# A new order of all steps in a fused two-block kernel, loop bounds read in three parts, and four more unread first products

## Chip, core and metric

One Trainium2 chip, one core. The time is the device time of the whole program in microseconds (us). The rows below come from one profiled execution; the median is over three unprofiled ones.

## What is computed

Two blocks, each a sequence mixer `s` gated by a mixture of experts `g`, on x of 16 x 256 x 128 (4096 tokens, float32):

```python
xn = layernorm(x)
s = linear_attention(xn)        # relu(q)+eps, relu(k)+eps, per sequence of 256
g = silu(moe0(xn))              # 8 experts of width 64, exact gelu, top 2, weights' sum
x = x + s * g
xn = layernorm(x)
s = ttt(xn)                     # per token: W -= LR*outer(2/d*(W k + b - v), k); out = W q + b
g = silu(moe1(xn))              # 8 experts of width 512, exact gelu, top 2, normalised
return x + s * g
```

In block 0 all eight experts are computed for every token. In block 1 each token goes only through the two experts chosen for it.

## The kernel before

**Groups.** The 4096 tokens are 32 tiles of 128, in 8 groups of 4. Each group passes through some fifty named steps. A step "3 kT" is group 3's share of the step kT; each engine has its own branch for it in its own `work(step, g)`, with the waits on semaphores that it needs, or nothing. Block 0: stats, roots, ln0, xt0, v, lg0, floor, sel, q, k, selT, kv, att, hid0 0 to 3 (dense experts), tok, y0, bias0, mix0. Block 1's mixer: ln1, norm1, xt1, resid, lg1, kT, qT, gram_n, diag and base and back (16 x 16 diagonal blocks of a triangular matrix go to HBM, are inverted on DVE and come back), half4, join4, half5, join5, turn, half6, join6 (the inverse by doubling: PE product, ACT copy into pn, PE product, copy back), gram_q, gram_x, then the chain u1, cross, u2, out, each a PE product and a copy that the next needs. "turn" is four transposes (L976) and one ACT copy (L1214); "half6" is L929 and the ACT copy L1198; "join6" L937 and L1204.

**Routing.** "rank", "slots" and "tok" give each token its two places in the HBM tensor `routed` (a region for each expert) and its weights. "send 0" to "send 3" are POOL's: each issues two indirect DMAs (L690) and waits first until the previous send of the group has landed. "7 send 0" waits for "9 tok" (weights_ready), since the gates of block 1 lag by two. "7 slots" also makes the table of loop bounds (L1601) on DVE. "U fill" is SP's: eight writes (L540) of filler rows behind each expert's tokens.

**Units.** Block 1's experts work on units of 256 routed rows. "U load k" is SP's load of a unit into a ring of four (it waits for unit k-4 to be done with: ring_free). "U hid k" is PE's hidden layer (L1025) and the transposition of unit k+1 (L1015), with DVE taking unit k+2 out of the ring (L1606). "U out k" is PE's output layer (L1048, in the loops L1037), ACT's four gelus of unit k+1 (L1235), DVE's scaling of the results, POOL's two indirect writes to `results` (L699). Units 0 to 7 are of fixed number and interleaved with the groups; the rest run in one loop per expert whose bounds each engine reads out of the table. PE reads its bounds two at a time in its "U hid" steps; ACT and DVE read all nine after "U out 6"; SP after the first pass. SP starts the load of unit 8 only when all sends of all groups have landed ("U sent", rows_landed) and the fill too. At the end the two results of each token are added by PE and the outputs stored.

**The order.** All engines walk one tuple, `ORDER` (L78 to L125). An engine works strictly in that order, so a step that waits holds up all behind it on the same engine. "idle" steps are four products of the identity into a bank that nobody reads (L742); eleven such steps stand in the order, and `FIRST_IDLE` (8) more products come before PE's first wait for weights (w_nat, L749).

Of the kernel before, what the change touches and what calls it, by code (L numbers as in the profile page):

```python
# [66 lines left out]
HALF = P // 2  # L67

GATES_LAG = 2
FIRST_IDLE = 8  # L70
IDLE = 4

WIDE = (0, 1, 6, 7)
# [2 lines left out]
ROOTS_TO = {0: 1, 1: 3, 3: 8}  # L76

ORDER = (  # L78
# [47 lines left out]

# [3 lines left out]
def two_block_kernel(nc, x, W_qkv, W_out, b_out, gate_w, w1_0, b1_0, w2_0, b2_0,  # L130
                     theta_K, theta_V, theta_Q, W0, b0, Wg, W1, b1, W2, b2, out):
    seqs, seq_len, D = x.shape
    E = gate_w.shape[1]
# [13 lines left out]
    FIRST_ALL = FIRST_UNITS * E  # L147
# [23 lines left out]
    with ctx:  # L171
        def sb(name, shape, dt=F32):
            return ctx.enter_context(nc.sbuf_tensor(name, shape, dt))
# [24 lines left out]
        cb0 = sb("cb0", [P, D])  # L198
# [19 lines left out]
        fill = sb("fill", [P, 2, HALVES, ROW])  # L218
# [34 lines left out]
        selT = [sb(f"selT_{i}", [P, P], BF16) for i in range(2)]  # L253
# [13 lines left out]
        send = [sb(f"send{i}", [P, CHOICES, TILES, ROW]) for i in range(2)]  # L267
# [7 lines left out]
        kT = sb("kT", [P, GW])  # L275
        qT = sb("qT", [P, GW])
# [154 lines left out]
        def unit_bounds(eng, first=0, last=E + 1):  # L431

            eng.wait_ge(table_ready, 1)
            return [eng.value_load(table[0:1, e:e + 1], min_val=FIRST_ALL, max_val=MAX_UNITS)
                    for e in range(first, last)]
# [299 lines left out]
        def _(pe):  # L735
# [3 lines left out]
            def idle_products(n, to=psC[:, 1, 0:P]):  # L739

                for _ in range(n):
                    mm(to, ident[:, :], ident[:, :], start=True, stop=True)  # L742

            pe.wait_ge(ident_in, 1)
            idle_products(FIRST_IDLE)
            pe.wait_ge(consts, 1)
# [346 lines left out]
        def _(act):  # L1093
# [148 lines left out]
            def unit_work(what, k=0):  # L1242
                if what == "first":
                    turned(0)
                elif what == "hid":
                    turned(k + 1)
                elif what == "gelu":
                    gelus(0, 0)
                elif what == "out":
                    gelus(k + 1, (k + 1) % E)  # L1250
                    if k == FIRST_ALL - 2:
                        bounds.extend(unit_bounds(act))

            bounds = []
            first_pass(act, work, unit_work)
# [11 lines left out]
        def _(dve):  # L1267
            v = nc.vector
# [369 lines left out]
            def unit_work(what, k=0):  # L1638
                if what == "first":
                    take(0)  # L1640
                    dve.wait_ge(S["xuT_ps"], 1)
                    take(1)
                elif what == "hid":
                    take_ahead(k)
                elif what == "out":
                    results_of(k, k % E, tiles(psB[:, 1, :], HALVES))
                    if k == FIRST_ALL - 2:
                        bounds.extend(unit_bounds(dve))

            bounds = []  # L1650
            first_pass(dve, work, unit_work)
# [45 lines left out]
```

## Time and profile before

| | us |
|---|---|
| median of 3 runs | 464.46 (461.81 to 465.18) |
| profiled execution | 466.61 |
| its span | 464.9 |
| PE, DVE, ACT, POOL busy | 418.2, 284.0, 215.4, 155.8 |
| mean granted clock of TensorE | 0.974 |

PE is the matmul engine, DVE VectorE, ACT ScalarE, POOL GpSimd, SP the queue that issues most DMAs. Times are microseconds from the start of the span. A timeline row gives start, duration, engine, line, operation and tiles, the count of merged instructions, and in brackets the idle time of the engine just before and what ended it. A float32 product of a 128-wide tile leaves two records. L12 is line 12 of the kernel.

### The profile page before, as it was taken

What the parts mean: (1) busy time and instruction counts of PE and PEld (TensorE: products, weight loads), DVE (VectorE), ACT (ScalarE), POOL (GpSimd) and SP (SyncE); (2) the same over time, 40 slices, a digit from 0 to 9 for tenths busy, and PEclk for the clock granted to TensorE, in tenths of its full rate; (3) what the DMA queues carried; (4) which work ended last, traced back from release to release, by engine and by line L of the source; (5) the groups of instructions that cost most, each with busy time, mean ns of one, the idle gap of its engine ahead of it and who ended that gap; (6) DMA issues with size and microseconds to landing.
All of it is one profiled execution on the core that took longest, in us unless ns stands there. A gap on an engine that the chain in (4) does not pass through costs nothing. (4 is left out here: it accounts for less than half of the span.)

```text
span 464.9 us, 9785 instructions
## 1 busy us (share of the span) xinstructions
PE 418.2 (90%) x2912; PEld 352.1 (76%) x2912; DVE 284.0 (61%) x1137; ACT 215.4 (46%) x525; POOL 155.8 (34%) x215
## 2 busy tenths in 40 slices
PE   6989988999999999998987989489799999999873
PEld 5967666878878889687776879388689899998631
DVE  2688889887887889888757476103133344343327
ACT  3274546555544746524425343214256555555512
POOL 6420014024034231533242014513344455555410
PEclk9999999999999999999999989779899999999998
DMA  7379011363172231121223213411122222222577
GB/s 187 105 147 168 8 37 35 75 196 87 33 199 75 83 75 38 42 77 43 63 55 91 50 32 91 117 45 45 47 61 66 70 69 75 68 70 70 147 253 216
DMA packets 63426, 40.80 MB, mean 88 GB/s; under 512 B 18324, under 2 KB 56088, under 8 KB 63384
## 3 DMA queue, kind: packets, MB, share of 16 engines
q1 hardware_dynamic: 58688, 31.27, 27.2%
q0 software_dynamic: 4352, 8.99, 5.8%
q8 instruction: 21, 0.34, 0.3%
q14 instruction: 21, 0.17, 0.1%
q10 hardware_dynamic: 344, 0.03, 0.1%
HBM read 21.78 MB, written 18.48 MB: 87 GB/s over the span
## 5 line engine op out<-in xcount | busy, mean ns | idle before, releaser
L690 POOL DMA_INDIRECT routed<-send,slot x64 | 65.0, 1015 | 128.3 <-DMA routed<-send,slot 50.6
L699 POOL DMA_INDIRECT results<-nat,y_to x72 | 70.1, 974 | 107.0 <-DVE nat L1634 85.1
L1025 PE MATMUL psA<-xuT,w_all 128*128 128x256 f32 x288 | 71.3, 391 | 3.7 <-ACT h1T L1235 3.2
L1235 ACT ACTIVATE h1T<-psA,b1T 128x256 f32<-128x256 f32 x144 | 62.8, 475 | 15.8 <-PE psB L1048 12.7
L1025 PEld LDWEIGHTS psA<-xuT,w_all 128*128 128x128 f32 x288 | 52.0, 195 | 12.5 <-ACT h1T L1235 3.6
L1606 DVE TENSOR_SCALAR xu<-ring 128x256 f32 (+1 forms) x38 | 11.3, 298 | 80.4 <-DMA ring<-routed 56.0
L1037 PE MATMUL psC<-w_all,h1T 128*128 128x128 f32 x464 | 57.1, 276 | 0.9 <-DVE nat L1618 0.9
L1037 PEld LDWEIGHTS psC<-w_all,h1T 128*128 128x128 f32 x464 | 54.5, 193 | 1.5 <-ACT h1T L1235 1.1
L1226 ACT ACTIVATE xuT<-psB 128x256 f32<-128x256 f32 x37 | 14.2, 384 | 63.4 <-PE psB L1015 38.2
L839 PE MATMUL psB<-xnT,w_l 128*128 128x512 f32 x64 | 34.2, 615 | 0.5 <-ACT selT L1155 0.5
L851 PE MATMUL psB<-w_l,hg0T 128*128 128x128 f32 x256 | 32.9, 281 | 0.0
L1166 ACT ACTIVATE hg0T<-psB,b1T 128x512 f32<-128x512 f32 x32 | 22.0, 689 | 22.7 <-PE psB L841 20.8
L851 PEld LDWEIGHTS psB<-w_l,hg0T 128*128 128x128 f32 x256 | 31.1, 192 | 1.8 <-ACT hg0T L1166 1.4
L841 PEld LDWEIGHTS psB<-selT,expert_of 128*128 128x128 bf16 x128 | 9.8, 98 | 18.2 <-issue 18.2
L1634 DVE TENSOR_SCALAR nat<-nat,y_wt 128x128 f32 (+1 forms) x72 | 17.5, 284 | 7.8 <-issue 4.8
L1173 ACT ACTIVATE gg<-psB,tok_w 128x128 f32<-128x128 f32 x32 | 9.1, 369 | 25.7 <-PE psB L852 21.9
L679 POOL COPY send<-send 128x512 f32<-128x512 f32 x8 | 4.9, 613 | 43.8 <-ACT send L1101 29.5
L742 PE MATMUL psC<-ident 128*128 128x128 f32 x104 | 16.7, 321 | 1.7 <-POOL ident L594 1.7
L742 PEld LDWEIGHTS psC<-ident 128*128 128x128 f32 x104 | 15.6, 234 | 1.7 <-POOL ident L594 1.7
L1321 DVE BATCH_NORM_STATS2 stats<-x_all 128x6 f32<-128x128 f32 x64 | 13.8, 278 | 3.9 <-DMA x_all<-in_L_attn_x_dram 3.7
L1101 ACT ACTIVATE send<-x_all,shift,rstd 128x128 f32<-128x128 f32 x32 | 13.2, 483 | 5.1 <-DVE shift L1338 5.1
L1048 PE MATMUL psB<-w_all,h1T 128*128 128x128 f32 x112 | 15.2, 295 | 0.0
(289 smaller groups left out, 865.0 us busy)
## 6 DMA issues: line engine op xcount, KB each, us to landing
ring<-routed SPq DMA_DIRECT2D x38, 130.0 KB
inv<-inv_room SPq DMA_DIRECT2D x8, 512.0 KB
w_all<-results SPq DMA_DIRECT2D x15, 256.0 KB, 4.5
routed<-ring SPq DMA_DIRECT2D x24, 130.0 KB, 6.1
n_room<-nT SPq DMA_DIRECT2D x8, 256.0 KB
w_all<-in_L_ffn_W_dram SPq DMA_DIRECT2D x1, 2048.0 KB
out_dram<-x_all SPq DMA_DIRECT2D x8, 256.0 KB, 2.3
results<-nat,y_to POOLq DMA_INDIRECT x72
```

Source lines behind the costliest of these rows:

```text
L690: pool.indirect_dma_start(routed[:, :], bass.IndirectOffsetOnAxis(ap=slot[par][:, c, t:t + 1], axis=0), send[par][:, c, t, :], None).then_ ...
L699: pool.indirect_dma_start(results[:, :], bass.IndirectOffsetOnAxis(ap=y_to[:, par, a:a + 1], axis=0), yw[:, par, a, :], None).then_inc(S[f ...
L742: mm(to, ident[:, :], ident[:, :], start=True, stop=True)
L839: mm(psB[:, j % 2, :], w, xT0[:, :], start=True, stop=False)
L851: mm(o, hg0T[:, j, col(t)], w2_l0[:, j, :], start=(j == 0), stop=False)
L1025: last = mm(psA[:, j // 2, (j % 2) * UNIT:(j % 2 + 1) * UNIT], w1_all[:, e, j * P:(j + 1) * P], xuT[:, :], start=True, stop=True)
L1037: last = mm(psC[:, a, 0:D], h1T[:, k, a * P:(a + 1) * P], w2_all[:, f * JF + k, :], start=(k == 0), stop=(k == JF - 1))
L1048: last = mm(psB[:, 1, col(a)], h1T[:, k, a * P:(a + 1) * P], w2_all[:, u % E * JF + k, :], start=(k == 0), stop=(k == JF - 1))
L1166: f(hg0T[:, j, :], psB[:, j % 2, :], ACT.Gelu, bias=b1T[:, HT + j:HT + j + 1]).then_inc(S["hg0_ready"], 1)
L1226: f(xuT[:, :], psB[:, 0, 0:UNIT], ACT.Copy).then_inc(S["xuT_ready"], 1)
L1235: f(h1T[:, j, :], psA[:, j // 2, (j % 2) * UNIT:(j % 2 + 1) * UNIT], ACT.Gelu, bias=b1T[:, n:n + 1]).then_inc(S["gelu_ready"], 1)
L1634: last = v.tensor_scalar(yw[:, mine, a, :], yb[:, a:a + 1, :], y_wt[:, a:a + 1], None, ALU.mult)
```

## The change

`FIRST_IDLE` is 12. ACT and DVE read three of the nine bounds after each of "U out 4", "U out 5" and "U out 6". `ORDER` is another permutation of the same entries; its start and its last part are shown, with the part in between left out. The hunk on the bounds is ACT's (L1251); DVE's (L1647) is the same with `dve`.

```diff
-FIRST_IDLE = 8
+FIRST_IDLE = 12
...
 ORDER = (
-    "0 stats", "0 roots", "0 landed", "0 ln0", "0 wout", "0 xt0", "0 wv", "0 weights", "0 products", "0 v",
-    "0 idle", "0 lg0", "1 idle", "0 floor", "0 sel", "0 q", "0 k", "1 stats", "2 idle", "0 selT", "2 stats",
-    "0 kv", "1 roots", "3 idle", "0 hid0 0", "0 hid0 1", "1 ln0", "3 stats", "0 att", "4 stats", "0 b2",
-    "0 hid0 2", "0 tok", "1 xt0", "4 idle", "1 v", "0 hid0 3", "1 lg0", "0 bias0", "2 ln0", "1 floor",
...
-    "7 floor", "4 send 3", "5 landed", "6 bias0", "3 cross", "5 copies", "7 sel", "6 hid0 3", "7 q", "7 tok",
-    "3 u2", "6 y0", "6 mix0", "3 out", "5 rank", "4 back", "5 slots", "5 kT", "7 selT", "5 send 0", "4 half4",
-    "5 gram_n", "4 join4", "4 half5", "5 diag", "6 ln1", "5 qT", "7 k", "4 join5", "5 gram_q", "6 norm1",
-    "6 xt1", "5 send 1", "4 turn", "7 kv", "4 half6", "4 join6", "4 u1", "5 base", "5 send 2", "7 att",
-    "5 back", "6 resid", "6 lg1", "5 gram_x", "4 cross", "5 send 3", "8 floor", "6 landed", "4 u2", "6 copies",
-    "7 hid0 0", "8 sel", "8 tok", "4 out", "6 rank", "6 slots", "6 kT", "7 hid0 1", "6 gram_n", "5 half4",
-    "6 diag", "5 join4", "6 send 0", "7 hid0 2", "5 half5", "7 bias0", "7 hid0 3", "6 send 1", "5 join5",
-    "6 base", "5 turn", "7 y0", "6 send 2", "5 half6", "6 qT", "5 join6", "6 send 3", "7 mix0", "5 u1",
-    "5 cross", "7 ln1", "6 gram_q", "6 back", "5 u2", "6 gram_x", "7 landed", "U load 0", "U load 1",
-    "7 norm1", "U load 2", "5 out", "U load 3", "7 xt1", "U first", "6 half4", "7 resid", "7 lg1", "U hid 0",
-    "7 kT", "6 join4", "7 gram_n", "U gelu 0", "9 floor", "7 copies", "6 half5", "9 sel", "7 diag", "U hid 1",
-    "6 join5", "U out 0", "U load 4", "7 base", "6 turn", "U hid 2", "6 half6", "6 join6", "6 u1", "U out 1",
-    "6 cross", "7 rank", "U load 5", "7 back", "7 slots", "U hid 3", "9 tok", "6 u2", "U out 2", "6 out",
-    "U load 6", "U hid 4", "7 send 0", "7 half4", "7 join4", "7 send 1", "U out 3", "7 send 2", "U load 7",
-    "7 half5", "7 send 3", "U sent", "7 qT", "7 join5", "7 gram_q", "7 turn", "7 half6", "7 join6", "7 gram_x",
-    "7 u1", "U fill", "U hid 5", "7 cross", "7 u2", "7 out", "U out 4", "U hid 6", "U out 5", "U hid 7",
-    "U out 6",)
+    "0 landed", "0 stats", "0 roots", "0 ln0", "1 stats", "0 wout", "0 wv", "0 xt0", "0 weights", "0 products",
+    "2 stats", "0 v", "0 lg0", "0 floor", "0 idle", "0 sel", "0 k", "0 q", "1 idle", "0 selT", "0 cb0",
+    "1 roots", "0 b2", "0 kv", "0 hid0 0", "1 ln0", "2 idle", "0 att", "3 stats", "0 hid0 1", "0 hid0 2",
+    "0 tok", "4 stats", "0 bias0", "3 idle", "1 xt0", "0 hid0 3", "5 stats", "6 stats", "0 copies", "1 v",
+    "0 y0", "1 lg0", "1 floor", "1 sel", "1 k", "1 q", "2 ln0", "7 stats", "4 idle", "1 kv", "5 idle",
...
+    "5 landed", "7 lg0", "3 u1", "6 hid0 3", "3 cross", "7 floor", "6 bias0", "5 copies", "7 q", "4 back",
+    "7 sel", "3 u2", "6 y0", "4 gram_x", "5 rank", "7 tok", "6 mix0", "3 out", "7 selT", "5 kT", "4 half4",
+    "5 slots", "5 gram_n", "5 send 0", "5 diag", "4 join4", "6 ln1", "5 qT", "4 half5", "7 k", "4 join5",
+    "6 norm1", "5 gram_q", "7 kv", "5 base", "4 turn", "5 send 1", "4 half6", "5 gram_x", "4 join6",
+    "5 send 2", "6 xt1", "5 send 3", "4 u1", "6 landed", "4 cross", "7 att", "6 resid", "5 back", "4 u2",
+    "6 qT", "6 lg1", "6 copies", "8 floor", "8 sel", "8 tok", "4 out", "6 rank", "6 slots", "6 kT", "7 hid0 0",
+    "6 send 0", "6 gram_n", "6 gram_q", "5 half4", "5 join4", "7 hid0 1", "5 half5", "5 join5", "6 send 1",
+    "7 hid0 2", "6 diag", "5 turn", "6 base", "7 hid0 3", "5 half6", "7 bias0", "6 send 2", "7 y0", "5 join6",
+    "7 mix0", "6 back", "5 u1", "6 send 3", "7 landed", "6 gram_x", "5 cross", "5 u2", "7 ln1", "U load 0",
+    "U load 1", "U load 2", "U load 3", "5 out", "7 norm1", "6 half4", "U first", "7 xt1", "6 join4",
+    "7 resid", "7 lg1", "U hid 0", "7 kT", "9 floor", "6 half5", "7 gram_n", "6 join5", "9 sel", "U gelu 0",
+    "U hid 1", "6 turn", "7 copies", "U out 0", "6 half6", "7 diag", "U load 4", "7 base", "U hid 2", "7 back",
+    "6 join6", "6 u1", "6 cross", "U out 1", "7 rank", "7 slots", "U load 5", "U hid 3", "6 u2", "U out 2",
+    "U load 6", "U fill", "6 out", "U hid 4", "7 half4", "U out 3", "7 join4", "U load 7", "7 half5", "7 qT",
+    "9 tok", "7 join5", "7 send 0", "U hid 5", "7 turn", "7 half6", "7 send 1", "7 gram_q", "7 join6",
+    "7 gram_x", "7 send 2", "7 send 3", "U sent", "7 u1", "7 cross", "7 u2", "7 out", "U out 4", "U hid 6",
+    "U out 5", "U hid 7", "U out 6",)
...
                     gelus(k + 1, (k + 1) % E)
-                    if k == FIRST_ALL - 2:
-                        bounds.extend(unit_bounds(act))
+                    if k > FIRST_ALL // 2 - 1:
+                        bounds.extend(unit_bounds(act, len(bounds), len(bounds) + (E + 1) // 3))
```

## Rows read from the trace of the kernel before

**Rows 1.** The page's granted clock of TensorE, in tenths, 40 slices of 11.6 us
```profile
PEclk9999999999999999999999989779899999999998
```

**Rows 2.** Windows: us; busy of PE, PEld, DVE, ACT, POOL; granted clock; DMA share; GB/s
```profile
60.00:80.00 20.00, 17.07 (x117) 12.45 (x116) 16.83 (x66) 11.70 (x29) 7.47 (x8) 1.00 0.13 38
...
295.00:300.00 5.00, 1.57 (x14) 1.18 (x12) 0.69 (x1) 0.38 (x1) 3.78 (x5) 0.75 0.44 130
```

**Rows 3.** Timeline of PE, ACT and DVE, units 7 to 11
```profile
324.64 1.99 PE L1025 MATMUL psA<-xuT,w_all 128*128 128x256 f32 x8 [0.32 <-issue]
...
331.05 3.23 PE L1025 MATMUL psA<-xuT,w_all 128*128 128x256 f32 x8 [2.41 <-ACT h1T L1235]
...
336.56 2.27 PE L1025 MATMUL psA<-xuT,w_all 128*128 128x256 f32 x8
...
340.67 2.15 PE L1025 MATMUL psA<-xuT,w_all 128*128 128x256 f32 x8
...
322.57 0.38 ACT L1226 ACTIVATE xuT<-psB 128x256 f32<-128x256 f32 x1 [1.64 <-PE psB L1015]
...
329.88 0.38 ACT L1226 ACTIVATE xuT<-psB 128x256 f32<-128x256 f32 x1 [4.57 <-issue]
...
323.39 0.29 DVE L1606 TENSOR_SCALAR xu<-ring 128x256 f32<-128x256 f32 x1 [1.99 <-DMA ring<-routed]
...
331.25 0.29 DVE L1606 TENSOR_SCALAR xu<-ring 128x256 f32 x1 [5.80 <-issue]
```

**Rows 4.** Timeline of PE, "U out 2" and "U out 4"
```profile
280.00 1.95 PE L1048 MATMUL psB<-w_all,h1T 128*128 128x128 f32 x16
...
313.61 1.95 PE L1048 MATMUL psB<-w_all,h1T 128*128 128x128 f32 x16
```

**Rows 5.** Timeline of PE, group 7's turn, half6, join6, and "U hid 5"
```profile
295.05 0.41 PE L976 MATMUL psD<-ident,inv 64*64 64x64 f32 x4
...
298.01 1.11 PE L929 MATMUL psD<-inv,nT 64*64 64x64 f32 x8 [2.55 <-issue]
...
302.44 1.08 PE L937 MATMUL psD<-inv,pn 64*64 64x64 f32 x8 [3.31 <-ACT pn L1198]
...
306.17 2.68 PE L1025 MATMUL psA<-xuT,w_all 128*128 128x256 f32 x8
```

**Rows 6.** Timeline of ACT, the copies of group 7's turn and half6
```profile
297.58 0.38 ACT L1214 ACTIVATE inv<-psD 64x256 f32<-64x256 f32 x1 [4.14 <-remote]
...
301.91 0.38 ACT L1198 ACTIVATE pn<-psD 64x256 f32<-64x256 f32 x1 [3.96 <-remote]
```

**Rows 7.** Timeline of SP and POOL, "U fill" and the last send's first half
```profile
293.13 11.08 SPq L540 DMA_DIRECT2D routed<-fill  x8
...
302.43 0.97 POOL L690 DMA_INDIRECT routed<-send,slot  x1 [1.83 <-DMA routed<-send,slot]
```

**Rows 8.** Timeline of DVE, the last write of the table
```profile
282.24 0.15 DVE L1601 CAST table<-bound_f 1x9 int32<-1x9 f32 x1
```

**Rows 9.** Timeline of PE, places at 24, 208 to 219 and 273 us
```profile
24.62 1.11 PE L821 MATMUL psA<-kv,q0T 128*128 128x129 f32 x8
...
208.65 1.10 PE L953 MATMUL psD<-inv,nT 128*128 128x64 f32 x8 [1.12 <-DVE inv L1572]
...
217.36 0.65 PE L937 MATMUL psD<-inv,pn 64*64 64x64 f32 x8 [0.56 <-ACT pn L1198]
...
219.02 1.93 PE L821 MATMUL psA<-kv,q0T 128*128 128x129 f32 x8
...
273.54 3.54 PE L1048 MATMUL psB<-w_all,h1T 128*128 128x128 f32 x16
```

**Rows 10.** Timeline of PE, the first products and the first transposes
```profile
1.73 3.78 PE L742 MATMUL psC<-ident 128*128 128x128 f32 x16 [1.73 <-POOL ident L594]
...
6.81 1.09 PE L749 MATMUL psD<-ident,nat 128*128 128x128 f32 x4 [1.30 <-DMA nat<-in_L_attn_W_dram]
```

**Rows 11.** Waits of POOL: total us, times, longest us
```profile
POOL routed L690 <- DMA routed<-send,slot: 50.6, 23, 6.2
```

More of the change, by code:

```diff
@@ L1646, in unit_work @@
                     results_of(k, k % E, tiles(psB[:, 1, :], HALVES))
-                    if k == FIRST_ALL - 2:
-                        bounds.extend(unit_bounds(dve))
+                    if k > FIRST_ALL // 2 - 1:
+                        bounds.extend(unit_bounds(dve, len(bounds), len(bounds) + (E + 1) // 3))
             bounds = []
```

51 rows, old and new, of the table ORDER are left out of this document.

## Prediction

> **What bounds the kernel now.** I read the page first, then TensorE (PE) in stretches, then the timelines at the places where it stood still. PE is busy 418.2 us of the span of 464.9, so all that a new order can win is in the other 46.7 us and in products at half clock. The clock line of the page [rows 1] shows where its granted clock fell: once near 220 us, once near 275, long near 300, once near 332. Up to 210 us VectorE (DVE) is full too: 16.83 us busy of 20 in 66 instructions, with a gap between any two dependent ones [rows 2], so a rearrangement there trades one full engine against the other. From 215 us DVE is light and PE alone sets the pace, so each PE stall and each stretch at half clock (1.2 instead of 2.4 GHz) is time lost. The worst stretch is 295 to 300 us, PE busy 1.57 of 5 us at a mean granted clock of 0.75 [rows 2]. After 336 us units follow each other without a gap; what is lost earlier is never won back, and what is won earlier is kept to the end.
>
> **Bounds in thirds.** ACT and DVE read nine loop bounds in one go after "U out 6". ACT's row at 329.88 has 4.57 us of idle ahead of it, 0.51 us a bound. PE starts its first products of units 8, 9, 10, 11 at 324.64, 331.05, 336.56, 340.67 [rows 3]: the last spacing, 4.11 us, is the steady one, the first two make 11.92 us where 8.22 would do. So the reading costs 3.7 us, of it 2.41 idle before 331.05, the rest the half clock that follows (eight records in 3.23 us there, 2.27 later). In thirds, three reads (1.5 us on ACT) fall behind outs 4, 5 and 6. Beside them in the kernel before ACT had 1.64 us of idle waiting for PE (row at 322.57), and DVE 1.99 us waiting for a ring load (row at 323.39), against 1.9 us for three reads there (5.80 us of idle for nine ahead of 331.25). So they hide. Gain 3.7 us; if the cover were gone from ACT twice, 2 x 1.5 us come back, so between 0.7 and 3.7. I take 3.7.
> The Trainium skill (Runtime: NRT & Kernel Launch, "Instruction fetch mechanics") puts one register load at about 200 ns; nine would be 1.8 us, less than the wait that covers them, and spreading them would then gain under 1 us. The ACT row with 4.57 us contradicts it, and the sum goes by the row.
>
> **The stall around 300 us.** Both orders hold the same steps between "U out 2" (PE at 280.00) and "U out 4" (313.61) [rows 4]. They took 33.6 us. At 298.01 and 302.44 PE stood 2.55 and 3.31 us [rows 5] for ACT copies. ACT's own rows have "remote" as releaser after 4.14 and 3.96 us of idle [rows 6]: PE's four transposes are put down as over at 295.46, yet the copy that needs only them starts at 297.58, 2.1 us late; the next is 2.8 us late. In just this stretch SP issues the eight filler writes ("U fill", 11.08 us, 293 to 304) while POOL scatters rows and results [rows 7]. I take it that the completion of everything is slow under that mixture; no row proves it. Then PE ran at half clock: L1025 took 2.68 us at 306.17 [rows 5] for 1.97 at full clock; over the products of 298 to 308 that sums to some 2.9 us. Together 8.8 us, of which some 1.1 us is the ordinary wait (0.5 us per dependent step) and stays: 7.7 at stake. The new order puts "U fill" directly behind "U load 6", the sends of group 7 behind it and not beside it, "U hid 5" ahead of "7 turn", and "7 gram_q" between half6 and join6. The fill then lies beside outs and hidden products (with two results scatters), which a 2 us delay stalls less. But "7 u1", "7 cross", "7 u2", "7 out" now follow with nothing between, +0.5 us. Ends: 7.7 us gained, or 0.5 lost if the lateness comes along. As the cause is inferred, I take about half: gain 4.0.
> What must move for it: the filler writes need the table, written at 282.24 [rows 8], so they can run from 283 to 294; "U load 7" is now queued behind them on SP, lands about 297.5 by a 3 us load, and DVE takes it in "U hid 5". Behind that take wait "7 gram_q", "7 cross" and "7 out" on DVE. In the new order I put PE's cross at about 302, so 4 us are spare.
>
> **The rest of the first pass.** Two further drops of the clock cost 1.6 us each: at 219.02 L821 takes 1.93 us in half-clock state for 1.11 at 24.62, and L1048 at 273.54 takes 3.54 for 1.95 at 280.00 [rows 4, 9]; ahead of each PE had several waits of half a microsecond (0.56 before 217.36). In the new order "5 gram_x" stands between "4 half6" and "4 join6", and "6 xt1" ahead of "4 u1", so two of three waits before 219 are covered and that drop should go: 1.6 + 1.0 - 0.5 for "4 cross" right behind "4 u1", 2.1 us. "5 qT" now stands between "4 join4" and "4 half5", where PE stood 1.12 us before 208.65 [rows 9]: 0.8. At 273 "U hid 2" moves between half6 and join6, but u1 and cross are bare: half of 1.6, 0.8. That is 3.7 us that I can name. Ahead of 210 us DVE is full, there I count nothing, though "1 xt0" has 1.5 us more of products ahead of it. What a whole new order breaks elsewhere I can't list; I take off a third: gain 2.5, between 6 gained and 4 lost.
> **Four more first products.** Eight are 16 records in 3.78 us from 1.73, about 0.45 us each, and end at 5.5; the weights release PE at 6.81 after 1.30 us of idle [rows 10]. Four more end at 7.3, 0.5 us late. ACT, which copies the transposed weights out, is still writing xn when they are done. Cost 0, at most 0.5; an earlier full clock could return up to 1 us.
>
> **Sum.** Profiled execution 466.6 us (span 464.9 and 1.7 around it): -3.7 - 4.0 - 2.5 - 0 = -10.2, so 456.4. The median of the runs shown, 464.46, lies 2.1 us below that execution; if it lacks part of the 300 us stall, the gain is smaller from a lower start, and the two offset each other. I leave 456.4.
>
> **Rivals.**
> *A, the lateness moves along and new stalls eat the rest.* The third term nought or negative, the 300 us stall back beside "7 half4" and "7 half5": only the bounds and about 1 us remain, 466.6 - 4.7 = 461.9. For it: the mechanism of "remote" is unproven, and an order that fits PE better in one place must take its cover from another. Against it: neither half6 nor join6 stands bare beside the fill any more. Chance 0.27.
> *B, slower: the last train of scatters holds unit 8.* "9 tok" now stands behind "7 qT", so "7 send 0" starts about 292: 280 plus some 9.5 us for "6 out" to "7 join4" at full clock and 2.5 us for tok's small instructions on DVE. A send costs 2 x 0.97 + 0.30 us of issue and 1.83 us until the one before has landed [rows 7]: 4.07. Four end at 308.3, before unit 4's results free the ring (about 309); turn 8 on PE is due at 315: unit 8's first products came 11.0 us after out 4 [rows 3, 4], its turn a hidden layer and a half earlier, some 2.5 us. But such waits reach 6.2 us and average 2.2 [rows 11]. Were all four as long as the longest, the rows land at 292 + 4 x 8.44 = 325.8, unit 8's load 3 us later, 14 us late: 466.6 - 10.2 + 14 = 470.4. It starts to hurt from 2.8 us a wait, and makes the kernel slower than before from 5.4. For it: DVE queues the results of unit 5 behind that take. Against: by then the fill is over. Chance 0.08.
> *C, everything named comes true.* 3.7 + 7.7 + 5, some clock at the start: 466.6 - 17 = 449.6 or so. Chance 0.12.
> *D, the change does not do what it says:* outs 4, 5 and 6 each read (8 + 1) // 3 = 3 bounds, nine in all, so it does; chance nil.
> The forecast keeps 0.53. Range 450 to 464.5: B and the ends of A and C are left out. A change of 1% (4.6 us) is about what a measurement tells from none: faster by over 1% (under 459.8) is the forecast nearly whole, C and a little of A, 0.63; within 1%: most of A and a part of the forecast, 0.28; slower 0.09.
>
> **What would show it.** Right: no 4.6 us idle on ACT between outs 6 and 8, and units 8 to 11 spaced about 4.1 us; no "remote" on ACT rows of group 7, turn to join6 within 3 us; clock line without the 5 in the slices near 300; out 4 about 7 us nearer to out 2 than 33.6. Wrong: a half-clock stretch in 285 to 295 beside the fill, SP's ring load of unit 8 released by the landing of rows, DVE's row of xu waiting long for unit 7's load, or more idle PE before 200 us than now.

## The result, and the profile after

The changed kernel takes 451.9 us (median of 5 runs, 451.13 to 454.52) against 464.46 for the kernel before (461.81 to 465.18): ratio 0.9745, 95% interval 0.9704 to 0.9786. That is 12.6 us less by the medians and 11.8 us by the ratio. Its profiled execution took 454.5 us with a span of 452.8, so 12.1 us less than that of before. The forecast was 456.4 us. A later section has the other half of the story: where the kernel before itself takes 455 us, the gain is only 5.7 us by the medians and 4.7 us by the ratio.

The page's line of the granted clock, against [rows 1]:

```profile
PEclk9699999999999999999999999979999999999997
```

The drops near 220, 275 and 332 us are gone, the long one near 300 is shorter, and there is a new one in the first 24 us. (At the start the line is a poor guide: it shows full clock for the kernel before, whose 16 records of unread products at 14.56 us took 3.42 us there; at full clock 16 take 1.95.) The timeline of PE at the places of [rows 4] and of the unit spacing of [rows 3]:

```profile
276.35 1.95 PE L1048 MATMUL psB<-w_all,h1T 128*128 128x128 f32 x16
...
305.71 2.77 PE L1048 MATMUL psB<-w_all,h1T 128*128 128x128 f32 x16
...
317.62 1.99 PE L1025 MATMUL psA<-xuT,w_all 128*128 128x256 f32 x8 [0.32 <-issue]
...
321.45 2.30 PE L1025 MATMUL psA<-xuT,w_all 128*128 128x256 f32 x8
...
325.60 1.89 PE L1025 MATMUL psA<-xuT,w_all 128*128 128x256 f32 x8
...
329.33 1.89 PE L1025 MATMUL psA<-xuT,w_all 128*128 128x256 f32 x8
```

Read them as milestones. "U out 2" comes 3.65 us earlier than before, "U out 4" 7.9 earlier, unit 8 7.0, unit 11 11.3, the end 12.1. So 3.65 us were won ahead of out 2, 4.3 between out 2 and out 4 (29.4 us for 33.6), and 4.3 in the spacing of units 8 to 11 (11.7 us for 16.0).

ACT's copies for group 7's turn and half6, against [rows 6]:

```profile
293.39 0.38 ACT L1214 ACTIVATE inv<-psD 64x256 f32<-64x256 f32 x1
...
294.54 0.38 ACT L1198 ACTIVATE pn<-psD 64x256 f32<-64x256 f32 x1 [0.76 <-PE psD L929]
```

Neither is late, and no row has "remote". (A row is called late below when it starts well behind the modelled end of the products that it waits for, and the profile names no engine that released it.) The filler writes ran from 282.62, and unit 7's load behind them was issued at 291.79:

```profile
282.62 8.98 SPq L540 DMA_DIRECT2D routed<-fill  x8
291.79 22.70 SPq L486 DMA_DIRECT2D ring<-routed  x3
```

(The second row merges three loads: only its start tells something.) What stayed is the bare end of group 7 (its last dependent steps, with nothing between them). PE's timeline has a wait before each of cross, u2 and out, and a half clock behind them:

```profile
298.82 0.68 PE L989 MATMUL psD<-upd,crossT 128*128 128x128 f32 x4 [1.09 <-ACT upd L1219]
300.02 0.72 PE L995 MATMUL psD<-res,inv 128*128 128x128 f32 x4 [0.52 <-DVE res L1576]
301.31 0.77 PE L1005 MATMUL psD<-m_out,xnT 128*128 128x128 f32 x2 [0.56 <-issue]
```

"7 out" and out 4 ran at half clock in this execution (L1048 2.77 us at 305.71 for 1.95 at 276.35). The profile of e2_order (below), which has the same order, shows no such drop there and 27.0 us from out 2 to out 4 (276.16 to 303.15). And the start got worse. DVE, then PE, for [rows 10] and what follows:

```profile
16.15 0.87 DVE L1321 BATCH_NORM_STATS2 stats<-x_all 128x6 f32<-128x128 f32 x4 [8.52 <-DMA x_all<-in_L_attn_x_dram]
```

```profile
20.34 1.73 PE L797 MATMUL psA<-wT,xnT 128*128 128x128 f32 x8 [3.48 <-DVE d_lg L1344]
...
33.35 0.64 PE L782 MATMUL psA<-ident,xn 128*128 128x128 f32 x4 [1.37 <-ACT s L1160]
```

"1 stats" now stands ahead of the gates of group 0 ("0 lg0") on DVE and waits for the load of x's other groups until 16.15 us. PE waits 3.48 us for them in consequence, and group 1's xt0 comes at 33.35 instead of 28.67. By group 0's kT, at 55 us, both kernels are level.

### The profile page after: what moved, and what is told of

Same layout as the page of the kernel before. It is cut to its first block, busy times and chain, and to the rows that moved or that the text cites. A ratio compares the mean times of both kernels' runs of the same rounds, so it can differ in the third digit from the quotient of the medians.

```text
span 452.8 us, 9800 instructions
## 1 busy us (share of the span) xinstructions
PE 414.3 (92%) x2920; PEld 349.0 (77%) x2920; DVE 285.4 (63%) x1137; ACT 213.5 (47%) x525; POOL 154.5 (34%) x215
## 4 chain that ended last, share of the span: by engine, by line
PE 48%; issue 20%; DVE 15%; DMA 6%; ACT 4%; SPq 2%; POOL 2%; DVEq 2%; POOLq 0%; ACTq 0%
PE psB L851 6%; PE psB L839 5%; PE psA L1025 5%; PE psB L1048 3%; DMA x_all<-in_L_attn_x_dram 2%; PE psC L1037 2%; PE psD L968 1%; DMA ring<-routed 1%; DMA routed<-send,slot 1%; PE psC L742 1%; PE psA L802 1%; DVE stats L1321 1%; PE psD L1005 1%; PE psA L797 1%; DVE x_all L1663 1%
## 5 line engine op out<-in xcount | busy, mean ns | idle before, releaser
L690 POOL DMA_INDIRECT routed<-send,slot x64 | 63.4, 991 | 127.0 <-DMA routed<-send,slot 56.2
L1025 PE MATMUL psA<-xuT,w_all 128*128 128x256 f32 x288 | 69.0, 382 | 2.1 <-issue 1.2
L1025 PEld LDWEIGHTS psA<-xuT,w_all 128*128 128x128 f32 x288 | 50.5, 190 | 10.3 <-issue 2.2
L1606 DVE TENSOR_SCALAR xu<-ring 128x256 f32 (+1 forms) x38 | 11.7, 307 | 68.4 <-DMA ring<-routed 64.2
L1173 ACT ACTIVATE gg<-psB,tok_w 128x128 f32<-128x128 f32 x32 | 9.1, 368 | 27.1 <-PE psB L852 23.5
L742 PEld LDWEIGHTS psC<-ident 128*128 128x128 f32 x112 | 17.2, 236 | 3.2 <-POOL ident L594 1.7
L742 PE MATMUL psC<-ident 128*128 128x128 f32 x112 | 18.0, 322 | 1.7 <-POOL ident L594 1.7
L1160 ACT ACTIVATE s<-psA,z 128x128 f32<-128x128 f32 x32 | 9.1, 367 | 13.5 <-DVE z L1491 13.5
```

What stands on the lines that cost most here:

```text
L690: pool.indirect_dma_start(routed[:, :], bass.IndirectOffsetOnAxis(ap=slot[par][:, c, t:t + 1], axis=0), send[par][:, c, t, :], None).then_ ...
L1025: last = mm(psA[:, j // 2, (j % 2) * UNIT:(j % 2 + 1) * UNIT], w1_all[:, e, j * P:(j + 1) * P], xuT[:, :], start=True, stop=True)
```

## Experiments

The kernel before was timed beside every set. It took 464.9 us in the first set and 464.05 in the last, but 455.1 and 455.5 in the two between. Each set ran on another chip (14, then 1, 4 and 6; for the runs of the result no chip is on record) and at another moment, so these runs can't tell a property of the chip from one of the moment. Ratios are always to the kernel before of the same set, and can differ by up to 0.3% from the quotient of the medians. I call the first condition P (before 464 to 465, also that of the prediction) and the second Q (before 455).

**One part each (P).** Bounds alone; order alone; and the order split ahead of "U load 0", where both orders have done the same 397 entries.

e1_thirds is the kernel before with this, in ACT and in DVE:

```diff
-                    if k == FIRST_ALL - 2:
-                        bounds.extend(unit_bounds(act))
+                    if k > FIRST_ALL // 2 - 1:
+                        bounds.extend(unit_bounds(act, len(bounds), len(bounds) + (E + 1) // 3))
```

> The kernel before with the bounds read in thirds and nothing else. Theory (the bounds' own term): units 8 to 11 come at 4.1 us spacing, nothing else moves, 3.7 to 4.3 us faster than the kernel before: 460.2 to 460.8 us, ratio about 0.991. Rival (the thirds only move the pause into three places where ACT and DVE are waited for): under 1 us faster, ratio above 0.998, and new idle on PE before units 6, 7 and 8.

461.09 us, ratio 0.9919 (0.9874 to 0.9965), 3.8 us less. PE's first products of units 8 to 11 and ACT's copy between out 6 and the loop:

```profile
322.48 1.99 PE L1025 MATMUL psA<-xuT,w_all 128*128 128x256 f32 x8 [0.32 <-issue]
326.32 2.27 PE L1025 MATMUL psA<-xuT,w_all 128*128 128x256 f32 x8
330.44 1.89 PE L1025 MATMUL psA<-xuT,w_all 128*128 128x256 f32 x8
334.17 1.89 PE L1025 MATMUL psA<-xuT,w_all 128*128 128x256 f32 x8
```

```profile
324.73 0.38 ACT L1226 ACTIVATE xuT<-psB 128x256 f32<-128x256 f32 x1 [1.57 <-PE psB L1015]
```

11.7 us for 16.0, and ACT's 4.57 us of idle are 1.57, ended by PE: the reads are hidden. The term stands. One late row is there too:

```profile
300.58 0.38 ACT L1198 ACTIVATE pn<-psD 64x256 f32<-64x256 f32 x1 [3.98 <-remote]
```

e2_order is the changed kernel with the bounds in one go again:

```diff
-                    if k > FIRST_ALL // 2 - 1:
-                        bounds.extend(unit_bounds(act, len(bounds), len(bounds) + (E + 1) // 3))
+                    if k == FIRST_ALL - 2:
+                        bounds.extend(unit_bounds(act))
```

> The changed kernel with all nine bounds read after out 6 again. Theory: loses what the thirds alone win, about 4 us, so 456 us and ratio 0.983. Rival (with another order the long read is hidden, or hurts more because PE comes sooner): 452 us or 458 us and more.

455.33 us, ratio 0.9794 (0.9702 to 0.9885). The order alone (with the 12 first products) is worth some 9.6 us here. The nine reads in one go cost less in its profile than in the kernel before: units 8 to 11 come in 14.0 us (314.28 to 328.26), as PE waits 2.41 us for them there too but no half clock follows.

e3_head is the changed kernel with the new order up to "U load 0" and the old one from there on (the two orders are named new and old here):

```diff
-ORDER = new
+ORDER = new[:new.index("U load 0")] + old[old.index("U load 0"):]
```

> New order up to the first unit load, old order behind it; thirds and 12 first products as changed. Theory: the new head is worth about 1 us at the end of it (group 7's xt1 came 1.0 us earlier in the profile of after), the thirds 4, and the stall around 300 us is back, since fill and sends are old: 459 to 460 us, ratio 0.990. Rival (the stall at 300 us belongs to chance, not to the place of the fill): no late copies in group 7's turn and half6, 453 to 455 us.

459.18 us, 0.9889 (0.9810 to 0.9969): only 1.4 us by the ratios (1.9 by the medians) better than the thirds alone, not resolved. Its ACT rows have the late copies back (its L1212 and L1196 are 1214 and 1198 of the other kernels):

```profile
296.93 0.38 ACT L1212 ACTIVATE inv<-psD 64x256 f32<-64x256 f32 x1 [4.15 <-remote]
...
301.24 0.38 ACT L1196 ACTIVATE pn<-psD 64x256 f32<-64x256 f32 x1 [3.92 <-remote]
```

e4_tail is the other way round:

```diff
-ORDER = new
+ORDER = old[:old.index("U load 0")] + new[new.index("U load 0"):]
```

> Old order up to the first unit load, new order behind it; thirds and 12 first products as changed. Theory: the tail holds nearly all of the order's gain (6 us by the profiles between group 7's xt1 and unit 8) and the thirds 4: 453 to 454 us, ratio 0.977. Rival (the head's 4.7 us loss at the start and its later gains matter more than the tail): 457 us or more if the head carries the gain, 450 us or less if the head as a whole costs.

451.84 us, 0.9701 (0.9624 to 0.9778): the changed kernel's time without its head. PE at out 2 and out 4 (its L1046 is 1048 of the others):

```profile
277.15 1.95 PE L1046 MATMUL psB<-w_all,h1T 128*128 128x128 f32 x16
...
304.23 1.95 PE L1046 MATMUL psB<-w_all,h1T 128*128 128x128 f32 x16
```

27.1 us for 33.6 in the kernel before (and 31.25 in e1_thirds, which has one late copy and not two). So the gain beyond the thirds is in the part behind "U load 0", about 9 us (461.09 to 451.84), and the new order of the 397 entries ahead of it brings nothing that can be told from the intervals.

**The place of the fill, the first products, the stats (Q).**

e7_fill_late is the changed kernel with "U fill" where the old order has it, behind "7 u1":

```diff
-    "U load 6", "U fill", "6 out",
+    "U load 6", "6 out",
...
-    "7 u1", "7 cross",
+    "7 u1", "U fill", "7 cross",
```

> The changed kernel with one entry moved: U fill stands behind 7 u1 again, as before. SP then issues the eight filler writes after U load 7, some 10 us later, beside the bare steps of group 7 and its sends. Theory (completions are late where fill and scatters run together and nothing covers PE): ACT rows with the releaser remote in group 7's turn, half6 or join6 or the chain behind them, PE idle 3 us or more there and a longer half clock, 3 to 8 us slower than the changed kernel: 455 to 460 us, ratio 0.980 to 0.990. Rival (the lateness came with PE's order alone, turn and half6 and join6 being bare): no late copy, within 1 us of the changed kernel, ratio 0.974.

450.25 us, 0.9890 (0.9817 to 0.9963), no late copy anywhere. In Q the kernel before has none either (b0_before, below), so this says nothing on P.

e8_fill_early is the kernel before with the opposite:

```diff
-    "U load 6", "U hid 4",
+    "U load 6", "U fill", "U hid 4",
...
-    "7 u1", "U fill", "U hid 5",
+    "7 u1", "U hid 5",
```

> The kernel before with one entry moved: U fill stands directly behind U load 6. Theory: the late copies of group 7's turn and half6 go, PE waits there 1.1 us in all for 5.9, the half clock near 300 us is shorter or gone; 4 to 7 us faster than the kernel before, 458 to 461 us, ratio 0.985 to 0.991. Unit 7's load comes behind the fill and does not delay DVE. Rival (order of PE's steps and not the fill is the cause): still late, ratio above 0.995; or the loss moves to unit 7's load, DVE's take of it over 5 us late, and the time stays.

455.72 us, 0.9992 (0.9957 to 1.0027), against the theory. The copies are in time (ACT's L1214 at 293.84 and L1198 at 294.99). But the kernel before took 455.1 us here, so there may have been nothing to cure, and the run leaves the question of the fill open.

e6_idle8 is the changed kernel with the old number of first products:

```diff
-FIRST_IDLE = 12
+FIRST_IDLE = 8
```

> The changed kernel with 8 first products. Theory: the first transposes start 0.2 to 0.5 us earlier, the clock rises later, as before, DVE still waits for the second x load until 16 us, so nothing reaches the end: within 1 us of the changed kernel, ratio 0.974. Rival (the four products change what clock the stretch from 7 to 25 us gets and so the end): 1 us or more apart, in either direction.

449.83 us, 0.9858 (0.9791 to 0.9924). The intervals of this and the unchanged kernel after (0.9898, below, on another chip) overlap. Each is 5 to 6 us wide, so four products more or fewer make no difference that can be told, and a difference of a microsecond or two would not show.

e5_stats is the changed kernel with "1 stats" and "2 stats" behind group 0's gates and q:

```diff
-    "0 ln0", "1 stats", "0 wout",
+    "0 ln0", "0 wout",
...
-    "0 products", "2 stats", "0 v",
+    "0 products", "0 v",
...
-    "0 q", "1 idle", "0 selT",
+    "0 q", "1 stats", "1 idle", "2 stats", "0 selT",
```

> The changed kernel with the stats of groups 1 and 2 back behind 0 q, as before, so that DVE does not wait for the second x load (8.52 us of idle) ahead of 0 lg0. Theory: the first 20 us are 4 us shorter on PE up to group 1's xt0, but by 60 us the changed kernel has made this up already (full DVE, idle products), so the end moves by less than 1.5 us: ratio 0.971 to 0.975. Rival (the 4 us are kept): 448 us, ratio 0.965.

450.02 us, 0.9859 (0.9764 to 0.9954). Group 1's xt0 came at 30.02 us instead of 33.79 in the kernel after of the same condition, out 2 at 273.9 instead of 275.4, and the span was 447.1 us instead of 448.2. So a microsecond may reach the end; the times do not resolve it.

**The two kernels themselves in condition Q.**

> The kernel before, unchanged, with a profile of its own. It took 464.5 and 464.9 us in two sets of runs and 455.1 in a third, on whatever chip these fell. Theory (the late copies near 300 us are a matter of chip and moment, and are what the 9 us are): where it takes about 464.5 its ACT rows of group 7's turn or half6 have the releaser remote and out 2 to out 4 takes 31 to 34 us; where it takes about 455, no such row and some 25.5 us. Rival (the whole program is slower on one chip): the 9 us are spread over the span. Ratio 1.000 in any case.

455.46 us, 0.9996 (0.9965 to 1.0027), so two kernels that are the same came out the same. Its profile (span 456.0) is what was missing. PE at out 2 and out 4, and ACT's two copies:

```profile
279.18 1.95 PE L1048 MATMUL psB<-w_all,h1T 128*128 128x128 f32 x16
...
305.96 1.95 PE L1048 MATMUL psB<-w_all,h1T 128*128 128x128 f32 x16
```

```profile
293.83 0.38 ACT L1214 ACTIVATE inv<-psD 64x256 f32<-64x256 f32 x1 [1.65 <-PE psD L976]
...
294.97 0.38 ACT L1198 ACTIVATE pn<-psD 64x256 f32<-64x256 f32 x1 [0.77 <-PE psD L929]
```

Out 2 to out 4 is 26.8 us for 33.6 in P; of the 8.9 us between the spans 6.8 are in this one place. So the kernel before is not slower all over in P: it has the late copies there and not here.

> The changed kernel, unchanged. Theory: its own time is about 450 to 452 us everywhere, so the ratio is 0.974 where the kernel before takes 464.5, and 0.988 to 0.991 where it takes 455 (the thirds' 3.8 us and 1 to 2 of order). Rival (the order's gain does not hang on the late copies): ratio 0.972 to 0.978 in both places.

449.86 us, 0.9898 (0.9844 to 0.9952): by the ratio 4.7 us (2.2 to 7.1), not 11.8; by the medians 5.7, not 12.6. Its own time is 2.0 us lower in Q than in P, that of the kernel before 9 us.

e9_fill_thirds is the kernel before with the edits of e1_thirds and e8_fill_early together.

> The kernel before with two edits, the bounds in thirds and U fill directly behind U load 6. Theory: the thirds give 3.8 us; if the kernel before takes 464.5 us here, the late copies go too and it comes to about 454 us (ratio 0.978); if that takes 455, the fill's place does nothing and it comes to about 451.5 us (ratio 0.992). Rival (the place of the fill never matters, lateness comes from PE's bare steps): 460.7 us in the first case, with remote rows.

450.11 us, 0.9903 (0.9866 to 0.9940). In Q the old order with two small edits is as good as the changed kernel, and by e8_fill_early one of the two is worth nothing: so the gain here is that of the thirds. (The thirds were not run by themselves in Q; this is by subtraction.) PE's first products of units 8 and 11 bear it out:

```profile
313.14 1.99 PE L1025 MATMUL psA<-xuT,w_all 128*128 128x256 f32 x8 [0.32 <-ACT h1T L1235]
...
324.44 1.89 PE L1025 MATMUL psA<-xuT,w_all 128*128 128x256 f32 x8
```

They are 11.3 us apart, as in a0_after (313.02 to 324.32), for 15.65 in b0_before (316.99 to 332.64).

The same profile settles something else. Up to "U load 6" its order is the old one, with the same 0.56 us wait ahead of 219 us, and yet neither of the two clock drops of [rows 9] is there:

```profile
218.01 1.06 PE L821 MATMUL psA<-kv,q0T 128*128 128x129 f32 x8
...
270.61 1.95 PE L1048 MATMUL psB<-w_all,h1T 128*128 128x128 f32 x16
```

It reaches out 2 at 275.44 us, like a0_after (275.42) and 3.7 us ahead of e8_fill_early (279.15), whose order is the same so far. So these drops come in some executions and not in others. Over all profiles (at 219 us without that of e10_gram, below, which has a step moved there), the one at 219 us is there in five of six with the old order at that place and in none of seven with the new; the one at 273 in four of seven with the old and in none of seven with the new.

**The fill's place in condition P.** The last kernel ran in P.

e10_gram is e9_fill_thirds with "5 gram_x" moved to between group 4's half6 and join6:

```diff
-    "4 half6", "4 join6",
+    "4 half6", "5 gram_x", "4 join6",
...
-    "6 lg1", "5 gram_x", "4 cross",
+    "6 lg1", "4 cross",
```

> The kernel before with three edits: the bounds in thirds, U fill directly behind U load 6, and 5 gram_x moved from behind 6 lg1 to between 4 half6 and 4 join6. Where the kernel before takes 464.5 us here, this decides what the earlier profiles could not: theory (the late copies go with the fill's place): no row with the releaser remote, out 2 to out 4 in 25 to 27 us, 451 us, ratio 0.971; rival (PE's bare order of turn, half6, join6 is what makes them late, in the new order they were covered): remote rows as in the head's run, 459 to 460 us. Where it takes 455: as with the two edits, 449 to 450 us, ratio 0.987 to 0.990; the third edit covers one wait of 0.5 us before the clock drop near 219 us and at best takes that drop away, 1 to 2 us.

460.39 us, 0.9926 (0.9890 to 0.9962): no better than the thirds alone. SP's fill was early, over by 295.9 us:

```profile
286.38 9.49 SPq L540 DMA_DIRECT2D routed<-fill  x8
```

yet ACT and DVE have late rows, two of them beside the fill and the third 6 us behind its end:

```profile
292.00 1.57 ACT L1235 ACTIVATE h1T<-psA,b1T 128x256 f32<-128x256 f32 x4 [4.99 <-remote]
292.07 0.42 DVE L1618 TENSOR_TENSOR nat<-psB,b_all 128x256 f32<-128x256 f32 x1 [2.71 <-remote]
...
302.05 0.38 ACT L1198 ACTIVATE pn<-psD 64x256 f32<-64x256 f32 x1 [3.97 <-remote]
```

The late copy and the lost time do not hang on the place of the fill. (The clock drop near 220 us is not there and out 2 came at 279.41 us for 280.0, 0.6 us; by e9_fill_thirds that drop can be missing without the moved gram_x too.) Nor does PE have to be idle for a completion to be late. PE's timeline beside these rows:

```profile
288.12 1.95 PE L1048 MATMUL psB<-w_all,h1T 128*128 128x128 f32 x16
289.91 1.06 PE L951 MATMUL psD<-inv,nT 128*128 128x128 f32 x8
290.80 1.02 PE L906 MATMUL psC<-xnT,wT 128*128 128x512 f32 x2
```

Out 3's products end at 290.07, DVE takes them at 292.07, and PE was busy until 291.8 between. What goes with the late rows is POOL's timeline:

```profile
286.19 0.97 POOL L699 DMA_INDIRECT results<-nat,y_to  x1 [5.52 <-DVE nat L1634]
287.47 0.97 POOL L699 DMA_INDIRECT results<-nat,y_to  x1 [0.31 <-issue]
288.74 0.97 POOL L690 DMA_INDIRECT routed<-send,slot  x1 [0.30 <-issue]
290.01 0.97 POOL L690 DMA_INDIRECT routed<-send,slot  x1 [0.30 <-issue]
293.41 0.96 POOL L690 DMA_INDIRECT routed<-send,slot  x1 [2.43 <-DVE nat L1634]
294.67 0.97 POOL L690 DMA_INDIRECT routed<-send,slot  x1 [0.30 <-issue]
295.95 0.97 POOL L699 DMA_INDIRECT results<-nat,y_to  x1 [0.30 <-issue]
297.22 0.96 POOL L699 DMA_INDIRECT results<-nat,y_to  x1 [0.30 <-issue]
298.49 0.96 POOL L690 DMA_INDIRECT routed<-send,slot  x1 [0.30 <-issue]
299.75 0.97 POOL L690 DMA_INDIRECT routed<-send,slot  x1 [0.30 <-issue]
```

Result scatters and sends follow each other without a wait: a train of four, then one of six, since a results scatter stands between two sends and hides the wait for the landing of each. The rows at 292.00 and 292.07 stand 1.0 us behind the end of the fourth, the copy at 302.05 1.3 us behind the end of the sixth. The kernel before has the same two trains (286.76 to 291.55, 293.28 to 300.60) and its late copies at 297.58 and 301.91: one in the middle of the second train and one 1.3 us behind its end, while the gelus of out 3, at 290.06, were in time. In e1_thirds the late copy (300.58) starts 0.1 us before the end of its train (300.68). What is the same in all four is the distance from half6's own products to its late copy: 3.90, 3.93, 3.87 and 3.92 us from start to start (before, thirds, head, gram), for 0.71 in b0_before. So the end of a train does not set the time at which the copy is released. In the new order all sends of group 7 stand between outs 3 and 4; each pair waits for the landing of the last, and after out 3 no results scatter comes between them:

```profile
290.54 0.97 POOL L690 DMA_INDIRECT routed<-send,slot  x1 [0.98 <-issue]
291.81 0.97 POOL L690 DMA_INDIRECT routed<-send,slot  x1 [0.30 <-issue]
294.91 0.97 POOL L690 DMA_INDIRECT routed<-send,slot  x1 [2.13 <-DMA routed<-send,slot]
296.18 0.96 POOL L690 DMA_INDIRECT routed<-send,slot  x1 [0.30 <-issue]
298.76 0.97 POOL L690 DMA_INDIRECT routed<-send,slot  x1 [1.62 <-DMA routed<-send,slot]
```

All four profiles in P with the old tail have trains and late rows (before, thirds, head, gram); all three in P with the new tail have neither (after, order, tail); none of the seven in Q has late rows, with trains or without. The three with the old tail in Q (before, fill_early, fill_thirds) have the same trains of four and six, and no late row. So late rows go with condition P and the old tail together, and the trains are one property of that tail. That is a correlation: no run broke up the trains and left all else. A rival is PE's own order, as half6 follows turn with PE idle between them; against it, it does so in the new order too (copies at 293.39 and 294.54), where "U hid 5" stands ahead of turn in place of "7 gram_q". That was not tested apart. Nor can the profile say whether the products or the news of them were late, since the ends of products are modelled. What the condition is, and what holds the copies back, stays open.

## Why the prediction was right, and where not

**What bounds.** Right: PE's idle and half-clock places set the time, and what was won ahead of unit 8 stayed to the end. Also right to count nothing for the stretch where DVE is full: by e3_head and e4_tail the whole head gives nothing that these runs resolve.

**Bounds in thirds, 3.7 us.** Right in size and mechanism: 3.8 us alone in P, ratio 0.9919; the spacing of the units gave 4.3. The difference is that 4.11 us was taken for the steady spacing, and the units come at 3.73 (325.60 to 329.33). In Q it is, by subtraction, the whole gain. By the Trainium skill (Runtime: NRT & Kernel Launch, "Instruction fetch mechanics") one register load takes about 200 ns. The estimate made from it, nine loads in 1.8 us and under 1 us to win, does not hold here: ACT's nine reads took 4.57 us and the thirds won 3.8. A read here is a load with a check of its range, so the page's figure for the load alone was not tested.

**The stall around 300 us, 4.0 of 7.7 us.** The size was about right, 4.3 us between out 2 and out 4 in the profile and 6.5 where the half clock stayed away (e2_order, e4_tail). The cause as put, the filler writes beside the scatters, was wrong: the step that failed is "I take it that the completion of everything is slow under that mixture" with the fill as its culprit. e10_gram moved the fill and kept the loss: 34.0 us from out 2 to out 4, and 460.39 us in all. So that the term came near was luck: half of a sum was taken for doubt, and the change removed the stall in P by something else in its tail. The scatters that it took apart are a candidate and no more. What was there to win is near 6.5 us in P and nought in Q. Q I had not thought of: the fact that a row has "remote" as releaser should have made me ask whether other executions have it. (The two orders do not quite hold the same steps between outs 2 and 4: "9 tok" lies there in the new one only.)

**The bare chain, +0.5 us.** Its waits came (1.09, 0.52, 0.56), but in the profiled execution they were followed by 6.8 us of half clock, which cost some 2.4 us more (29.4 us from out 2 to out 4 for 27.0 in e2_order). The five runs spread over 3.4 us, and the profiled one is the slowest: the clock there differs from run to run. Most of the 2.6 us from the profile to the median may be this.

**The rest of the first pass, 2.5 us.** Out 2 came 3.65 us earlier. The two named clock drops are gone in the profile after. But e4_tail reaches out 2 at 277.15, with the old head and a clock drop at 219, so most of it lies behind "U load 0" (the rearranged turn, half6, join6 of group 6), and of the 2.9 us that I counted in the head at the steps of group 4 some 0.6 to 0.8 us are there at out 2 (e3_head against e1_thirds, after against e4_tail). The term was near by its sum and not by its places. In Q nothing of it can be seen: the old order in e9_fill_thirds had neither drop and reached out 2 together with the changed kernel, and both took the same time (450.11 and 449.86 us). That the new order prevents the drops is likely by the counts above and not shown.

**Four more products, 0.** Right: not to be told from 8. "1 stats" ahead of a load was overlooked: 8.5 us of DVE idle, 4.7 us at group 1's xt0, level again at 55 us.

**The sum.** -10.2 forecast, -12.6 measured, -12.1 from profile to profile: the doubt subtracted from the second term is enough to explain these 2.4 us. Of the 4.5 us between 456.4 and 451.9 the other 2.1 are the start: the sum began at the profiled execution (466.6 us) and not at the median. Rival B did not come: the last send was issued by 304.8 us, before out 4 ended, and its waits were 1.6 to 2.1 us. Rival A's gain of 4.7 us is what came in Q, but not by its road: there was no stall at 300 us to move along.

## What to carry to other kernels

Price a stall only after asking whether every execution has it: here some 7 of the 12.6 us gained were a stall that the kernel before has in one condition and not in another, and two profiles of the same kernel, with spans 8.9 us apart, told more than any theory. The same holds for a drop of the clock: one profile more of the old order would have shown that it need not come. Split a long permutation at a point where both orders have done the same steps: two runs then say which half works, and here the last 72 of 469 entries did all that these runs resolve. Register reads that stall an engine on the path are cheap to spread over waits that are there anyway.

## What was not expected of the hardware

ACT and DVE went on 2 to 3 us behind the modelled end of PE's products in the same stretch of the old order in four profiles (before, thirds, head, gram), and never in three other profiles with it (before, fill_early, fill_thirds in Q). The waiting instructions themselves took no longer than elsewhere (the copies 0.38 us, POOL's scatters 0.97). It coincides with four and more indirect DMAs issued back to back, but the three profiles without it have these too, and the late copy of half6 comes a fixed 3.9 us behind the start of its products wherever the train ends. And 0.5 us waits in a row of dependent products can be followed by 6.8 us at half clock in one execution and by none in another of the same order (27.0 us against 29.4 from out 2 to out 4).
